# An attention stage with its value products as 64-column float32 products, and its scores three tiles ahead

## What is computed

```python
x = x + 0.5 * ffn(layernorm(x)); x = x + attn(layernorm(x)); x = x + 0.5 * ffn(layernorm(x))
# attn: 4 batches of 512 positions, 16 heads, 64 + 64 query/key columns, 64 value columns
q_pe, k_pe = apply_rope(q_pe, cos, sin), apply_rope(k_pe, cos, sin)      # the rotary halves
attn = jnp.einsum('bhqd,bhkd->bhqk', query_states, key_states) * SOFTMAX_SCALE
attn = jax.nn.softmax(attn.astype(jnp.float32), axis=-1)
out = jnp.einsum('bhqk,bhkd->bhqd', attn, value_states)
return out.transpose(0, 2, 1, 3).reshape(b, s, NH * V_DIM) @ wo
```

## Time and profile before

| | us |
|---|---|
| median of three runs (lowest, highest) | 1192.55 (1191.17, 1195.83) |
| the profiled execution | 1193.56 |
| its span, first to last instruction | 1191.7 |
| TensorE matmul busy | 1043.2 (88%) |
| VectorE busy | 824.7 (69%) |
| ScalarE busy | 616.5 (52%) |
| GpSimd busy | 502.7 (42%) |

### The profile page before, as it was taken

How to read it: one execution, slowest core, us unless ns; L and a number is a source line. 1 busy time by engine, 2 the same in 40 slices (tenths; PEclk the granted TensorE clock), 3 DMA queues, 4 the chain that set the end, 5 groups by cost and what they waited for, 6 DMA issues and landing times.

```text
span 1191.7 us, 24657 instructions
## 1 busy us (share of the span) xinstructions
PE 1043.2 (88%) x6200; PEld 867.2 (73%) x6201; DVE 824.7 (69%) x1750; ACT 616.5 (52%) x1340; POOL 502.7 (42%) x464
## 2 busy tenths in 40 slices
PE   4579999995646999999999999999989729999995
PEld 4557888784634888888888888888778627887884
DVE  5365556643765999999999999999835455565552
ACT  1243334321125888888888888888810123343321
POOL 2542333333223555555555566655412532333332
PEclk9999999998677999999999999999999859999998
DMA  9844445332100011111010110011464463454231
GB/s 238 248 163 98 99 105 137 61 55 48 36 1 1 10 36 37 35 35 35 35 35 35 35 35 28 27 34 35 142 218 146 129 221 98 106 143 111 44 52 15
DMA packets 71562, 95.41 MB, mean 80 GB/s; under 512 B 9600, under 2 KB 48640, under 8 KB 71296
## 3 DMA queue, kind: packets, MB, share of 16 engines
q1 hardware_dynamic: 57216, 78.04, 21.3%
q0 software_dynamic: 14304, 16.87, 7.8%
HBM read 64.37 MB, written 34.43 MB: 83 GB/s over the span
## 4 chain that ended last, share of the span: by engine, by line
PE 47%; DMA 26%; issue 11%; DVE 4%; POOL 4%; ACT 1%; POOLq 1%; SPq 0%; DVEq 0%; ACTq 0%
DMA out<-shared,small 12%; DMA x_after_moe<-shared,small 12%; PE bank L1535 9%; PE bank L1551 7%; PE bank L1525 6%; PE bank L1552 5%; PE bank L1526 5%; PE bank L1527 5%; PE bank L1514 2%; POOL rows_by_expert L529 2%; PE bank L1515 2%; PE bank L1616 1%; PE bank L1476 1%; PE bank L1352 1%; PE bank L1354 1%
## 5 line engine op out<-in xcount | busy, mean ns | idle before, releaser
L810 ACT ACTIVATE shared<-bank,small 128x512 f32<-128x512 f32 x256 | 175.8, 687 | 57.9 <-DVE small L1184 55.5
L1184 DVE TENSOR_REDUCE small<-bank 128x1 f32<-128x512 f32 x256 | 175.2, 685 | 37.8 <-PE bank L1527 27.6
L1214 DVE TENSOR_TENSOR split_rows_and_inner<-bank,shared_split 128x512 fp32r<-128x512 f32 x256 | 174.7, 682 | 7.0 <-ACT shared_split L819 5.0
L762 ACT CAST split_rows_and_inner<-bank 128x512 fp32r<-128x512 f32 x78 | 45.7, 586 | 246.7 <-PE bank L1337 246.7
L1535 PE MATMUL bank<-constants,shared 128*128 128x128 f32 x1024 | 155.2, 274 | 0.9 <-ACT shared L810 0.9
L1551 PE MATMUL bank<-shared_split 128*128 128x256 f32 x512 | 144.4, 304 | 5.5 <-DVE shared L1208 2.2
L819 ACT CAST shared_split<-bank 128x512 fp32r<-128x512 f32 x256 | 147.3, 575 | 1.0 <-PE bank L1535 1.0
L1354 PE MATMUL bank<-expert_weights_low,split_rows_and_inner 128*128 x312 | 144.1, 462 | 0.0
L1356 PE MATMUL bank<-expert_weights_high,split_rows_and_inner 128*128 x312 | 143.0, 458 | 0.0
L1551 PEld LDWEIGHTS bank<-shared_split 128*128 128x128 f32 x512 | 96.3, 188 | 56.4 <-issue 27.3
L1552 PE MATMUL bank<-split_rows_and_inner,shared_split 128*128 128x256 f32 x512 | 132.8, 282 | 0.0
(11 more groups left out here) (191 smaller groups left out, 2483.8 us busy)
## 6 DMA issues: line engine op xcount, KB each, us to landing
expert_weights<-L_ffn_w_kernel SPq DMA_DIRECT2D x32, 512.0 KB, 4.6
shared<-rows_by_expert SPq DMA_DIRECT2D x78, 129.0 KB, 2.1
expert_weights<-L_ffn_wo_kernel SPq DMA_DIRECT2D x16, 512.0 KB, 6.1
shared<-inverse_sums SPq DMA_DIRECT2D x64, 128.0 KB, 2.9
attended_transposed<-shared SPq DMA_DIRECT2D x32, 256.0 KB, 2.7
expert_weights<-attended_transposed SPq DMA_DIRECT2D x2, 2048.0 KB, 10.2
shared<-attended_transposed SPq DMA_DIRECT2D x2, 2048.0 KB, 10.6
rows_by_expert<-empty_rows SPq DMA_DIRECT2D x23, 129.0 KB, 3.5
```

The lines of the kernel that those rows point to most:

```text
L810: nc.scalar.activation(prob[k % 2], bank[k % 4][:, :], ACT.Exp, bias=negmax[:, k % 8:k % 8 + 1], accum_out=psum[par][:, k % 8:k % 8 + 1]). ...
L1184: V.tensor_reduce(negmax[:, k % 8:k % 8 + 1], bank[k % 4][:, :], AX.X, ALU.max, negate=True).then_inc(max_ready, 1)
L1214: V.tensor_tensor(pTl[k // 2 % 2][:, :, at], bank[4 + k % 2][:, :].rearrange("p (c n) -> p c n", c=GT), pTh[k // 2 % 2][:, :, at].bitcast( ...
```

## The change

- **Values.** The value product is now plain float32: `attend` has, for each chunk of 128 keys, one product per head with the 64 value columns as weights. Head 0 goes to partitions 0 to 63 of bank 6, head 1 to 64 to 127, in turns. Tiles are now in the order head 0, head 1 of the same query block (`tile`), so that four tiles make half a pair. The products come in two runs of eight per pair: `attend(p - 1, .., 1)` at k = 1 and `attend(p, .., 0)` at k = 5. `pTh`, `pTl` and the split values are gone; `pT` holds plain float32 for two heads and two halves.
- **Copies.** Each transposed tile is copied once: tiles 0, 1, 4, 5, 7 by VectorE, tiles 2, 3, 6 by ScalarE (`copy_pT`). Bank 6 is copied once per pair, whole, by VectorE (`take_output`). GpSimd's addition is gone; its copy of the values is one of 128 by 256 in place of two of 128 by 512.
- **Lead.** Scores are issued three tiles ahead (`AHEAD = 3`), exponentials two ahead of the transposes into four `prob` buffers.
- **Queries.** Parts 0 and 1 of pair p + 2 are issued at k = 3 and 6, part 2 at k = 0 of the pair before; ScalarE rounds at k = 0 and 1, VectorE's low parts come at k = 1, `rope_sum(p + 2)` closes GpSimd's pair. Query weights have two buffers and are loaded three pairs ahead.

The core of the diff:

```diff
             def attend(...)
-                cols = slice((1 - hh) * HD, (1 - hh) * HD + P)
-                for c in (2 * piece, 2 * piece + 1):
-                    mm(bank[6][:, at], vcur[par][:, 0, c, cols], pTh[half % 2][:, c, :], start=(c == 0), stop=False)
-                    last = mm(bank[6][:, at], vcur[par][:, 1, c, cols], pTl[half % 2][:, c, :], start=False, stop=(c == GT - 1))
+                wait_pT(pe, p, (3, 6)[half])
+                wait_pT(pe, p, (1, 7)[half])
+                for c in range(GT):
+                    for hh in range(2):
+                        last = mm(bank[6][hh * HD:(hh + 1) * HD, at], vcur[par][:, c, :], pT[half][hh][:, c, :],
+                                  start=(c == 0), stop=(c == GT - 1))
...
             def pair(p, par):
                 for k in range(8):
                     transposed(p, k, first)
-                    if k < 6:
-                        scores(p, par, k + 2)
+                    if k + AHEAD < 8:
+                        scores(p, par, k + AHEAD)
                     elif not last:
-                        scores(p + 1, 1 - par, k - 6)
+                        scores(p + 1, 1 - par, k + AHEAD - 8)
...
+                    if k == 0 and not first and not last:
+                        queries(p + 1, 1 - par, 2)
+                    if k == 1 and not first:
+                        attend(p - 1, 1 - par, 1)
+                    if k == 2 and not first:
                         if not last:
                             pe.wait_ge(qz_low, p * 2 + 4)
                         inverse_transpose(p - 1, 1 - par)
+                    if k == (4 if first else 3) and not among(p, NPAIR - 2, NPAIR - 1):
+                        queries(p + 2, par, 0)
+                    if k == 5:
+                        attend(p, par, 0)
                     if k == 6 and not among(p, NPAIR - 2, NPAIR - 1):
-                        queries(p + 2, 0)
-                    if k > 1:
-                        attend(p, par, k // 2 - 1, k % 2, first)
-                    elif not first:
-                        attend(p - 1, 1 - par, 3, k)
+                        queries(p + 2, par, 1)
```

More of the change, by code:

```diff
@@ L258, in build @@
         kEl, kOl = (split_area(wlo, k * B * S, [B, S]) for k in range(2))
-        vh, vl = (split_area(wlo, 2 * B * S + k * B * GT * HD, [B, GT, HD]) for k in range(2))
         m = F32_SHARED
@@ L353, in head_pairs @@
                 pair(p, p % 2)
-            with eng.Fori(0, (NPAIR - 6) // 2) as i:
+            with eng.Fori(0, (NPAIR - 8) // 2) as i:
                 for v in range(2):
                     pair(i * 2 + 4 + v, v)
-            for p in (NPAIR - 2, NPAIR - 1):
+            for p in range(NPAIR - 4, NPAIR):
                 pair(p, p % 2)
@@ L640, in _ @@
-            load_weights(1, 1)
+                nc.gpsimd.tensor_copy(values[:, g, :, :], keys[:, :, HD:2 * HD]).then_inc(v_kept, 1)
+            pool.wait_ge(v_kept, B)
+            load_values(0, 0, None)
+            load_weights(1, 1, None)
             rope_sum(0)
             rope_lower(0, 0)
+            load_weights(2, 0, 1)
             def pair(p, par, half):
                 last = among(p, NPAIR - 1)
-                if not last:
-                    rope_sum(p + 1)
+                if among(p, 0):
+                    rope_sum(1)
@@ L657, in pair @@
-                if not last:
-                    load_values(p + 1, 1 - par, None if among(p, 0) else p * 4)
+                    load_values(p + 1, 1 - par, None if among(p, 0) else p * 2)
+                if not among(p, NPAIR - 2, NPAIR - 1):
+                    rope_sum(p + 2)
             for p in range(4):
                 pair(p, p % 2, p // 2)
-            with pool.Fori(0, (NPAIR - 6) // 2) as i:
+            with pool.Fori(0, (NPAIR - 8) // 2) as i:
                 for v in range(2):
@@ L830, in queries_rope @@
                 nc.scalar.copy(qh[par][hh][rows_], rope[rows_]).then_inc(rope_high, 1)
-            def take_output(p, par, hh):
-                rows_ = slice(hh * HD, (hh + 1) * HD)
-                act.wait_ge(o_psum, p * 4 + hh * 2 + 2)
-                if hh == 0 and not among(p, 0, 1):
-                    act.wait_ge(att_ready, p - 1)
-                nc.scalar.copy(raw[par][rows_], bank[6][rows_, :]).then_inc(raw_sb, 1)
             def take_inverse(p):
@@ L1501, in flat, with queries @@
                 return v.rearrange("p a n -> p (a n)")
-            def queries(p, part):
+            def queries(p, par, part):
                 src = flat(cq[:, bass.ds(p // PAIRS, 1), :])
@@ L1513, in queries @@
                     pe.wait_ge((ropeA_sb, ropeB_sb)[part - 1], p + 1)
-                mm(bank[7][:, :], wch[:, part, :], src, start=True, stop=False)
-                mm(bank[7][:, :], wcl[:, part, :], src, start=False, stop=True)\
+                mm(bank[7][:, :], wch[par][:, part, :], src, start=True, stop=False)
+                mm(bank[7][:, :], wcl[par][:, part, :], src, start=False, stop=True)\
                     .then_inc((qa_psum, qb_psum, qz_psum)[part], 1)
             def scores(p, par, k):
-                hh, qt = k // 4, k % 4
+                hh, qt = tile(k)
                 if k == 0:
@@ L1563, in pair @@
                     transposed(p, k, first)
[L1564 to L1565 removed]
+                    if k + AHEAD < 8:
+                        scores(p, par, k + AHEAD)
                     elif not last:
[L1567 to L1570 removed]
+                        scores(p + 1, 1 - par, k + AHEAD - 8)
+                    if k < 3 and first:
+                        queries(1, 1, k)
+                    if k == 0 and not first and not last:
[3 more added lines that the diff above has]
+                    if k == 2 and not first:
                         if not last:
@@ L1593, in _ @@
             inverse_transpose(NPAIR - 1, 1)
-            for piece in range(2):
-                attend(NPAIR - 1, 1, 3, piece)
+            attend(NPAIR - 1, 1, 1)
             def second_route(g, part):
```

220 lines of the change are left out of this document (101 added, 119 removed).

## The result

| | us |
|---|---|
| before, median of 4 runs (lowest, highest) | 1194.19 (1191.17, 1196.5) |
| changed kernel, median of 4 runs | 1173.84 (1171.91, 1176.84) |
| ratio, 95% interval | 0.9848 (0.9831 to 0.9865) |
| the profiled execution; its span | 1171.91; 1170.1 |
| predicted; range | 1273; 1168 to 1305 |

The change makes the kernel 1.5% faster. The forecast was 1273 us, slower; the time is that of the rival "the halves overlap", which was priced at 1174 and given a chance of 0.20.

A forecast was written before the change was run, and what follows sets the result against it. TensorE's own work was taken to fill 14.42 of 15.49 us per pair, a full VectorE making the rest. 9.20 + 1.38 + 6.83 + 0.48 + 0.10 = 17.99 us, 2.50 more, times 32 = 80 us: 1273 us, range 1168 to 1305.

The forecast's parts named there:

- the halves overlap: Value products on different column halves run side by side, 0.213 us each: 14.9 us per pair, 1174 us; chance 0.20.
- What bounds the kernel: Attention pair: TensorE's own work fills 14.42 of 15.49 us; the other 1.07 are waiting, made by a full VectorE.
- The price of a product: Value products in `attend`: 0.427 us each as in L1461, so 6.83 us per pair in place of 3.84.
- The second support: Full-width float32 products of L1616: 0.215 us per record, 0.43 per product, the same price as half width.
- The argument against the overlap: L1461: 32 records in 16 steps of two, no single record at either end, still 0.427 us per product.
- One behind the other: Value products: a product's two records no longer start together, 0.854 us each, 13.7 per pair, 1492 us; chance 0.08.
- Change between widths: Edges of the two value-product runs on TensorE: four per pair at 0.12 us, 0.48 us; ends 0 and 0.96.
- The chain behind the run: Bank 6 copy, inverse and its transpose after a run: 0 to 0.2 us; rival 0.8 per pair, 1295 us, chance 0.10.
- The lead of three tiles: Scores issued ahead on TensorE, with early queries and doubled buffers: adds no instruction, only covers; 0.1 us waiting counted per pair.
- The rival's slow end: Side-by-side value products with the present waiting of 1.07 us per pair kept: 1190 us.

The follow-up runs named there:

- Series 3 and 5: Changed kernel plus 24 unused float32 products per series, 64 columns, always the lower column half, with 128 rows (3) or 64 rows (5): 0.43 us per product.
- series 2: Changed kernel plus 24 unused float32 products of 128 rows by 64 columns, output in the two partition halves in turns: 0.22 us per product.

## Why the prediction was wrong, step by step

- **What bounds the kernel.** Right in its numbers: 14.42 us of TensorE's own work and 1.07 of waiting in a period of 15.49. Wrong in the cause of the waiting. I gave it to a full VectorE; relieved by 2 us per pair, VectorE gave back 0.17. The 15.2 us were a sum of durations, which counts overlaps twice; by the window VectorE was busy for 14.3 of 15.49. And 0.23 of the 1.07 were a wait for GpSimd's low parts of the queries, which I had not seen.
- **The price of a product, 0.427 us.** This is the step that failed, and it alone turned the sign: with the 0.216 us that the changed kernel shows, my sum is 14.62 us, 28 us less than before instead of 80 more. It took L1461's distance at the clock that the column named, 1.00. At that place TensorE ran at 1.2 GHz; at 2.4 GHz the same instructions step by 0.213 us per product. The second support, that full width costs the same 0.43, then looked like an agreement of two rows and was one row at half clock and one product without a partner. The rest of the sum was near: with the price built in, 1263 us.
- **The argument against the overlap.** "32 records fall into 16 steps of two" was read as two records of one product. Series 3 and 5 show that records of one half never run together, so the twos were of two products, and the row for the rival lay in my own rows. No single record is left at either end because two products start together, first record beside first record (88.800 and 88.807 us in series 2). The rule of the Trainium skill that I had set beside it, in TensorEngine Tiling (Array Packing), Key Properties, holds here for float32: two tiles of 64 columns run in parallel, 0.22 us per product against 0.43 in one of them.
- **One behind the other, 0.854.** The two records of a product do run one behind the other, but at 0.216 us each, with another product beside them. The 0.854 did not happen; it too rested on the half clock, by a 64-column transpose that was compared with full-width records at the other level.
- **Change between widths, 0.48 us per pair.** Measured 2 x 0.29 = 0.58. Near, though the rows for it lay in the slow stretch.
- **The chain behind the run.** 0 to 0.2 us, as counted; it becomes dear when the run is cut in two.
- **The lead of three tiles, counted at nothing but cover.** Mis-sized: without it the change gains nothing (1192 us). The overlap rival came to 14.9 us and 1174 by 0.4 us of waiting, which were about 0.15, and an edge cost that was 0.10 too low; and the few microseconds ahead of the stage and behind it do not come from its period. The time agrees partly by luck. (The rival's slow end, 14.47 + 1.07 = 15.54 us, is 1194 us and not 1190.)

## What to carry to other kernels

Before a duration of TensorE is carried from one place of a trace to another, compare an instruction of the same shape at both places; a clock column that says full speed is no proof, above all at the start. Plain float32 products of 64 columns cost half each if two independent ones are issued in turns to the two column halves; here they took the same TensorE time as the float32r products with split operands, and replaced a path over two engines by one copy. Judge how full an engine is by the window and not by the sum of its durations, and look for the wait that each order of instructions makes. And where a change bunches TensorE's work, count the lead in time and not in tiles: here it paid only with a third tile.

## What the runs showed of the hardware

- Float32 products of 256 columns at 2.4 GHz: 0.43 to 0.44 us with full width, with 64 rows by 128 columns, and with 64 columns in one half; 0.22 us in turns between two column halves, at 128 or 64 rows, or between two row halves with 64 by 64 weights and two banks.
- TensorE starts a product in a free half ahead of earlier ones that wait for the other half: by the starts of single records, head 1's first ran beside head 0's fifth of eight.
- A run in the other width costs about 0.29 us beside its streaming, for runs of four, eight and 16 products alike.
- The clock column of these traces said 1.00 from the start, while products stepped as at 1.2 GHz until 80 to 89 us.
